# The second router's correction in three reduced-precision passes instead of one single-precision product

## The reference

```python
def _L1_cond_ref(x, language_ids, W, Wr, A, B):
    logits = x @ Wr.T + bias            # 8 experts, 5.0 added for the sequence's language
    gates = top-2 of logits, softmax over the two
    h = einsum('btd,erd->bter', x, A)   # 8 experts x rank 16 = 128 values a token
    return x @ W.T + 2.0 * einsum('bter,bte,eor->bto', h, gates, B)

def _L1_ffn_ref(x, W_base, b_base, W_router, A, B):
    logits = x @ W_router.T
    combine = top-2 of softmax(logits), divided by their sum
    h = einsum('nd,erd->ner', x, A)
    return x @ W_base.T + b_base + 2.0 * einsum('ner,eor->no', h * combine[..., None], B)

x = x + _L0_ffn_ref(_L0_cond_ref(x, ...), ...)
x = x + _L1_ffn_ref(_L1_cond_ref(x, ...), ...)
```

## Time and profile before

| | |
|---|---|
| median of 3 runs | 988.67 us (988.07 to 990.8) |
| profiled execution, its own time | 988.7 us |
| its span | 986.9 us |
| TensorE busy | 979.6 us, 99% |
| VectorE busy | 591.9 us, 60% |
| ScalarE busy | 464.3 us, 47% |
| granted TensorE clock, mean | 1.00 |

### The profile page before, as it was taken

One profiled execution on the slowest core, in us unless ns is written; L12 is line 12 of the kernel. 1 busy time (PEld: TensorE's weight loads), 2 busy tenths in 40 slices (PEclk: granted clock), 3 DMA queues, 4 the chain that ended last, 5 costly groups with the idle time before them and its releaser, 6 DMA issues.

```text
span 986.9 us, 14042 instructions
## 1 busy us (share of the span) xinstructions
PE 979.6 (99%) x4787; PEld 829.0 (84%) x4787; DVE 591.9 (60%) x969; ACT 464.3 (47%) x854; POOL 256.5 (26%) x244
## 2 busy tenths in 40 slices
PE   8999999999999999999999999999999999999998
PEld 7888888888888888888888888888888899888886
DVE  5654586788784423596333299233278488786762
ACT  5645566555761333572333374233357264535342
POOL 5232232654400631400531230171140460000000
PEclk9999999999999999999999999999999999999999
DMA  8997866666977976877887786986789650606132
GB/s 279 359 321 285 310 215 233 250 224 246 340 268 257 293 222 196 268 224 259 298 277 197 225 269 235 316 281 194 195 268 324 235 193 22 234 33 224 65 107 86
DMA packets 121487, 230.12 MB, mean 233 GB/s; under 512 B 12613, under 2 KB 12613, under 8 KB 121161
## 3 DMA queue, kind: packets, MB, share of 16 engines
q1 hardware_dynamic: 118880, 220.81, 67.1%
q0 software_dynamic: 2400, 8.41, 2.3%
q10 hardware_dynamic: 136, 0.01, 0.0%
HBM read 165.74 MB, written 63.44 MB: 232 GB/s over the span
## 4 chain that ended last, share of the span: by engine, by line
PE 94%; DVE 2%; DMA 2%; issue 1%; ACT 1%; POOL 0%; DVEq 0%; SPq 0%; ACTq 0%
PE bank L1820 92%; DMA ab<-in_ab_table,row_i 1%; PE bank L1844 1%; PE bank L1981 1%; DMA t_raw<-t_scratch 1%; ACT xs_hi L1126 0%; DMA slot_i<-in_slots 0%; DVE hg L1644 0%; DVE greater L1624 0%; DVE xs_lo L1529 0%; ACT bank L1277 0%; DVE wins L1620 0%; DVE rank L1627 0%; DVE greater L1618 0%; POOL ab L776 0%
## 5 line engine op out<-in xcount | busy, mean ns | idle before, releaser
L1820 PE MATMUL bank<-cop_hi,wring 128*128 128x512 f32 x1234 | 380.7, 389 | 0.3 <-issue 0.3
L1820 PEld LDWEIGHTS bank<-cop_hi,wring 128*128 128x128 f32 x1234 | 231.6, 188 | 49.0 <-ACT bank L1041 0.9
L1820 PE MATMUL bank<-cop_lo,wring 128*128 128x512 f32 x616 | 239.7, 389 | 0.0
L1820 PE MATMUL bank<-op_hi,wring 128*128 128x512 f32 x560 | 173.7, 389 | 0.0
L1472 DVE TENSOR_TENSOR v<-bank,p7s 128x512 f32<-128x512 f32 x44 | 30.4, 691 | 200.3 <-PE bank L1820 200.3
L1820 PEld LDWEIGHTS bank<-cop_lo,wring 128*128 128x128 f32 x616 | 115.6, 188 | 23.9
L1820 PEld LDWEIGHTS bank<-op_hi,wring 128*128 128x128 f32 x560 | 105.1, 188 | 21.9
L1820 PE MATMUL bank<-op_lo,wring 128*128 128x512 f32 x280 | 108.9, 389 | 0.0
L1072 ACT ACTIVATE s<-bank 128x512 f32<-128x512 f32 x44 | 26.3, 597 | 115.7 <-PE bank L1820 115.7
L1458 DVE TENSOR_TENSOR op_lo<-h,op_hi 128x512 fp32r<-128x512 f32 x100 | 72.6, 743 | 3.9 <-ACT op_hi L1029 3.7
L821 POOL TENSOR_TENSOR h_t<-h,h 128x512 f32<-128x512 f32 x20 | 27.6, 1382 | 160.4 <-DVE h L1494 160.4
(11 more groups left out here) (227 smaller groups left out, 1926.0 us busy)
## 6 DMA issues: line engine op xcount, KB each, us to landing
wring<-wgu_scratch SPq DMA_DIRECT2D x231, 256.0 KB, 3.0
wring<-wd_scratch SPq DMA_DIRECT2D x140, 256.0 KB, 5.2
wgu_scratch<-wring SPq DMA_DIRECT2D x77, 256.0 KB, 3.6
x_raw<-in_x SPq DMA_DIRECT2D x32, 256.0 KB, 7.3
c_scratch<-c_out SPq DMA_DIRECT2D x32, 256.0 KB, 2.8
c<-c_scratch SPq DMA_DIRECT2D x32, 256.0 KB, 4.2
xs_raw<-x_scratch SPq DMA_DIRECT2D x16, 512.0 KB, 5.7
out<-res SPq DMA_DIRECT2D x32, 256.0 KB, 2.1
```

Source lines behind the costliest of these rows:

```text
L1820: return e.matmul(out_ap, lhs, rhs, start=start, stop=stop, skip_group_check=True)
```

## The change

`ra2` is split like the other 136 columns: ScalarE writes `ra2_hi`, VectorE `ra2_lo`. `route_h` multiplies the halves of the transposed gated h, which `out_h1` needs anyway, by the halves of `ra2` in three passes. The copy `hg1t` is gone with its semaphore and its place in memory. `route_h` waits for `ring_freed("th", 0, t)`, which is the end of VectorE's low half, where it waited for ScalarE's copy; in tile 0 it waits for the low half of `ra2` as well.

```diff
-    ra2 = work("ra2", [LH], F32)
+    ra2_hi = work("ra2_hi", [LH], F32R)
+    ra2_lo = work("ra2_lo", [LH], F32R)
...
-    hg1t = work("hg1t", [TOK], F32)
...
         def weight_product(i):
             left, right = ring_bank("left", i, 0), ring_bank("right", i, 0)
-            own = xt_hi[:, i, LH:2 * LH] if i < KC else ra2[:, :]
+            own = xt_hi[:, i, LH:2 * LH] if i < KC else ra2_hi[:, :]
...
             if i == 0:
-                if t > 0:
-                    e.wait_ge(pe_ring, ring_full("rh", t - 1, 1))
-                else:
-                    e.wait_ge(t_stored, DMA * 4 * NS)
-                e.activation(hg1t[:, :], bank[:, :], ACT.Copy).then_inc(hg1t_done, 1)
                 if u > 1:
                     e.wait_ge(pe_acc, l_mark(u - 2, 1, "c12"))
...
             e.wait_ge(m2_hi_done, 2 * i + 1)
-            if i < KC:
-                e.tensor_tensor(xt_lo[:, i, LH:2 * LH], right[:, D - CUT:D - CUT + LH],
-                                plain(xt_hi[:, i, LH:2 * LH]), ALU.subtract).then_inc(xt_lo_done, 1)
+            own_hi, own_lo = ((xt_hi[:, i, LH:2 * LH], xt_lo[:, i, LH:2 * LH]) if i < KC else
+                              (ra2_hi[:, :], ra2_lo[:, :]))
+            e.tensor_tensor(own_lo, right[:, D - CUT:D - CUT + LH], plain(own_hi),
+                            ALU.subtract).then_inc(xt_lo_done, 1)
...
         def route_h(t):
-            e.wait_ge(hg1t_done, t + 1)
+            u, j = divmod(t, 2)
+            e.wait_ge(*ring_freed("th", 0, t))
             if t == 0:
-                e.wait_ge(*ring_freed("left", KC, 0))
+                e.wait_ge(xt_lo_done, KC + 1)
             for half in range(2):
                 bank = take_ring("rh", t, half)
                 for c2 in range(2):
-                    c = 2 * half + c2
-                    done = mm(bank[:, c2 * LH:(c2 + 1) * LH], hg1t[:, c * P:(c + 1) * P], ra2[:, :], True, True)
+                    tok = slice((2 * half + c2) * P, (2 * half + c2 + 1) * P)
+                    done = mm3(bank[:, c2 * LH:(c2 + 1) * LH], hg1_hi[u % 2][j][:, tok], hg1_lo[u % 2][j][:, tok],
+                               ra2_hi[:, :], ra2_lo[:, :], True, True)
                 done.then_inc(pe_ring, 1)
```

More of the change, by code:

```diff
@@ L323, in build @@
     hg_done = [sem(f"hg_done{i}") for i in range(2)]
-    hg1t_done, hgt_hi_done = sem("hg1t_done"), sem("hgt_hi_done")
+    hgt_hi_done = sem("hgt_hi_done")
     def nth(t, m=KC - 1):
```

## The result

The changed kernel takes 999.81 us at the median of 4 runs (998.47 to 1001.4), the kernel before 988.84 us (988.07 to 990.8) beside it: a ratio of 1.0111, 95% interval 1.0096 to 1.0126. It is slower by 11.0 us where 7.7 were forecast. Slower was right, and so were the two causes in the sum, the passes and the wait. The time lies within the range of 994.5 to 1008.7, but above the forecast's own 994.5 to 998. The missing 3.3 us have a place of their own: the fourth rival, a fall of TensorE's clock at the long wait, took place, and cost 2.7 to 3.3 us where 1.6 us stood.

What follows compares the result with a forecast made beforehand. TensorE was taken to bound the kernel, busy 979.6 of 986.9 us. Passes 3.7, tile 7's wait 3.2 net and tile 1's wait 0.8 added to 988.7 gave 996.4 us; own range 994.5 to 998, with two rivals 994.5 to 1008.7.

Steps and rivals of the forecast that it cites:

- the passes: Correction on TensorE: 96 narrow passes at 115 ns replace 64 single-precision instructions at 115 ns, +3.7 us.
- the fourth rival: TensorE's clock falls in the pause of tile 7: 1.6 us more, 998.0 us; chance 0.09.
- Rival 3: Correction's 96 instructions: no load floor, 57 ns a pass, -1.9 us; with the waits +2.1, 990.8 us; chance 0.07.
- The first rival: Correction: a narrow pass costs a whole single-precision product, 230 ns; +14.7 us, with waits 1007.4 us; chance 0.27.
- the 81 ns: Skill's pace for load and matmul pairs of 128 columns; for the correction's passes 7.8 us, +0.4 us.
- The wait of tile 7: TensorE's correction of tile 7 waits for VectorE's low half: 3.95 us lost, 3.2 us net.
- The wait of tile 1: TensorE's correction of tile 1 waits for VectorE's low half: 0.8 us lost.
- What comes back: TensorE's old waits after 953.07 (0.39 us) and before the transposes at 964.68 (0.3 us) vanish.
- VectorE will have done both in time: After tile 7's pause, the line 1552 addition and tile 7's router are ready; 0.4 and 0.3 us return.
- The clock: TensorE at the 4 us pause of tile 7: no fall taken; 1.6 us lost if it falls.
- The added subtraction: VectorE's extra 136-column subtraction, 0.3 us, before TensorE's third chunk at 800.99: put at nothing, at most 0.1 us.

Runs made afterwards that it cites:

- the wait alone: Kernel before, single-precision product kept, with the correction also waiting for the end of VectorE's low half: 996.94 us, ratio 1.0072.
- the filled pause: Changed kernel with 14 thrown-away products of 512 columns issued just before the wait of tile 7's correction: 998.13 us, ratio 1.0089.
- the low half first: Changed kernel with VectorE's low half of tile 7 ahead of tile 6's router, and ScalarE's copy ahead of its exponential: 993.01 us, ratio 1.0041.
- the one with 64 columns: Changed kernel with the three-pass correction cut to its first 64 columns, the other 72 left out: 999.14 us, run once.
- the changed kernel once more: The changed kernel, unaltered, run again beside a later set of the kernel before: 998.77 us, ratio 1.0098.

## Why the prediction was right, and where it was short

**The passes: right.** Forecast 3.7 us from 96 x 115 ns. The step is 112 ns, and in each tile the first is 62 ns, which the sum did not count; measured, 3.2 us. But how the floor was come by was luck. The prediction read it off the transposes (109 ns) and the product that is removed (115 ns), and neither row shows one: both are single-precision instructions, and two streams of 128 and of 136 columns make 107 and 114 ns (2 x 128 x 0.42, 2 x 136 x 0.42). For the product the first steps above show it. For the transposes no run varied the width, but their first step behind a wide pass (at 963.27 before the change) is 109 ns too. The true floor of 111 to 112 ns happens to lie between the two. Rival 3 had the right reading of the 115 ns, and the wrong conclusion that there is no floor. The first rival (230 ns), with a chance of 0.27, fails outright, and it alone had pushed the upper end of the range to 1008.7. The Trainium skill's rule of P/1.2 ns a load (TensorE: Matmul & The Clock Gate, section on LDWEIGHTS), an estimate of 107 ns, comes within 5 ns of the step, and the 81 ns of that page's section on the back-to-back issue gap are not seen at 136 or at 64 columns.

**The wait of tile 7: right.** Forecast 3.95 us before anything comes back; measured 3.76 and 0.11 more in the step behind it, 3.9 us, in the tile and behind the queue that were named.

**The wait of tile 1: right.** Forecast 0.8 us; 0.7 us in the changed kernel (1.1 us for the tile, less 0.4 for its passes) and 0.8 us in the wait alone. The other six tiles show none.

**What comes back: half right.** The 0.39 us after 953.07 are gone. The 0.3 us before the last transposes were counted as well and stay: 976.49 - 975.99 = 0.50 us between the starts in the changed kernel, as before, and in the filled pause and the low half first too. The step that failed is "VectorE will have done both in time". VectorE's own timeline shows why:

```profile
966.76 0.19 DVE L1597 TENSOR_TENSOR diff<-lx,top 128x32 f32<-128x32 f32 x1
972.04 0.19 DVE L1602 TENSOR_REDUCE z_sum<-expo 128x4 f32<-128x32 f32 x1 [5.08 <-ACT expo L1156]
```

The router of tile 7 stands 5.1 us for ScalarE's exponential, which lies in ScalarE's queue behind a copy that TensorE paces (line 1280, until 971.89). In the kernel before, this wait was 2.7 us. So VectorE's lead is eaten in ScalarE's queue, and TensorE meets the same wait wherever it was held up before. I had followed one queue where two take part.

**The clock: the step that failed.** The prediction says "I take no fall, since TensorE was busy without a break before", gave the fall a chance of 0.09 and 1.6 us. The fall came every time, and cost 2.7 to 3.3 us where a trace shows it. Its chance was too low: a pause longer than any in the trace is no argument for the state of things within it. And the price was bounded by the wrong stretch. I took the 3.2 us of slow passes at the start of the program; at the pause the lower level held for 6.8 us in each of the four profiled executions with the fall, and half of 6.8 is 3.4. How much of them falls into the pause, where it costs nothing, differs (nothing, or 1.1 to 1.2 us). With this price in place of none and the returned 0.3 us taken out, the prediction's own terms give 3.2 + 3.9 - 0.4 + 0.7 + 3.3 = 10.7 us, and 10.2 with 2.8 us for the clock; the traces have 10.6 and 10.1.

**The added subtraction: thin cover, as said.** The third chunk of tile 0's first router now meets it: the two steps at 801.93 and 802.10 are 0.17 and 0.23 us where 0.126 is normal, so 0.15 us are lost, against nothing in the sum and 0.1 us as its bound. It lies before 814 us and so is not in the 10.6.

No version was found that beats the kernel before. Three narrow passes cost 336 ns a product and the two single-precision instructions 230, and the copy that the change saves was hidden.

## What to carry to other kernels

A product with its own stationary operand has a least price, 111 ns here, however few columns it moves; so three passes in place of two instructions is a loss below about 336/(4 x 0.42) = 200 columns, whatever the count of the passes says. That figure is an estimate from the prices of this case (336 ns for three passes at the floor, four streams of 0.42 ns a column in single precision); no run has a product of that width in both forms. When a change moves a wait from one engine's result to another's, list the waits tile by tile: six of eight can be harmless and the one at the seam of the schedule costs more than all the passes. And price a pause of TensorE, where it bounds the kernel, twice, once for its length and once for the clock behind it; a rearranged queue that removes the pause gets back both. Last, a row that fits a floor may fit its columns as well: before a floor is read off it, ask what the columns of that type alone would cost.

## What the runs showed of the hardware

- At a pause of 3.6 to 3.7 us the clock fell in each of the four profiled executions that had one, and the 17 runs with it all have 0.998 or less over the span; the mean is 1.0 in all 10 runs where the pause was filled or the low half came first, and with a pause of 2.4 us in 2 of 6.
- The lower level held for 6.8 us in each of the four. It began within 0.2 us behind the end of the pause in two of them (the changed kernel, and the one with 64 columns) and 1.1 to 1.2 us before its end in the other two (the changed kernel once more, and the wait alone).
- At the lower level the narrow pass steps by 213 ns, the upper level's 112 ns nearly doubled, so the least price goes with TensorE's clock.
- Single precision meets the same floor as the reduced type, 111 ns at 64 columns; its 115 ns at 136 columns are two streams of its columns.
- The start of the program differs from run to run. In the profiled execution of the changed kernel the first product passes, from 6.46 us, stepped at the pace of the lower level until 9.6 us; in the one before they did not the earlier trace rows. The record of the granted clock does not show it (the last row, from the table of stretches), so the means over the span do not count it:

```profile
6.46 0.77 PE L1816 MATMUL bank<-xa_hi,w_hi 128*128 128x512 f32 x1 [0.72 <-DVE w_lo L1384]
7.02 0.63 PE L1816 MATMUL bank<-xa_lo,w_hi 128*128 128x512 f32 x1
7.45 0.63 PE L1816 MATMUL bank<-xa_hi,w_lo 128*128 128x512 f32 x1
...
5.00:10.00 5.00, 4.28 (x10) 2.83 (x10) 2.77 (x4) 3.11 (x5) 4.48 (x9) 1.00 1.02 374
```

At 10 us that is 1.3 us, and from 20 us on 1.0, a part of the spread of some 3 us that the kernel before and the changed one have here.
